# Grouping the value matmuls of two chunks in the attention loop of a one-core Macaron block

## What is computed

```
x = x + 0.5 * ffn(layernorm(x))      # 256 -> 1024, butterfly, gelu, butterfly, -> 256
Q, K, V = einsum('bsd,hkd->bhsk', layernorm(x), WQ / WK / WV)
scores = where(causal, einsum('bhqd,bhkd->bhqk', Q, K) / sqrt(16), -inf)
x = x + einsum('bhsv,hdv->bsd', softmax(scores) @ V, WO)
x = x + 0.5 * ffn(layernorm(x))
```

## Time and profile before

| | |
|---|---|
| median of 3 runs | 2121.79 us |
| the profiled execution, device time | 2122.12 us |
| its span from first to last instruction | 2120.3 us |
| mean granted TensorE clock | 0.988 |
| PE busy | 2033.0 us (96%) |
| DVE busy | 1680.3 us (79%) |
| ACT busy | 1350.4 us (64%) |
| POOL busy | 259.0 us (12%) |
| attention loop | 462.4 to 1884.2 us (first and last scores) |

### The profile page before, as it was taken

The page is one execution under the profiler, slowest core; times in us unless marked ns, Lnnn a source line. Parts: engine busy times, 40 slices in busy tenths (PEclk is TensorE's granted clock), DMA queues, the critical chain, the costliest instruction groups (busy, mean ns, idle before and its releaser), DMA issues.

```text
span 2120.3 us, 58107 instructions
## 1 busy us (share of the span) xinstructions
PE 2033.0 (96%) x23960; PEld 1207.5 (57%) x23960; DVE 1680.3 (79%) x3588; ACT 1350.4 (64%) x1592; POOL 259.0 (12%) x723
## 2 busy tenths in 40 slices
PE   1699999989999999999999999999999999999999
PEld 1476666555555555555555555555555555568887
DVE  6734444459999999999999999999999999635562
ACT  2423222238888888888888888888888888763222
POOL 8300000001111111111111111010110111100000
PEclk8799999999999999999999999999999999999999
DMA  7011211121211111111111111111111111101110
GB/s 202 22 48 47 86 52 51 47 61 44 51 42 45 41 43 49 42 46 41 44 47 42 46 43 44 46 42 46 43 44 45 42 46 33 50 24 60 60 40 21
DMA packets 89976, 104.19 MB, mean 49 GB/s; under 512 B 21264, under 2 KB 52592, under 8 KB 89456
## 3 DMA queue, kind: packets, MB, share of 16 engines
q1 hardware_dynamic: 89008, 100.23, 16.6%
q0 software_dynamic: 704, 0.25, 0.2%
HBM read 70.54 MB, written 29.36 MB: 47 GB/s over the span
## 4 chain that ended last, share of the span: by engine, by line
PE 92%; DVE 4%; ACT 2%; issue 1%; SPq 1%; DMA 0%; ACTq 0%; DVEq 0%
PE PS L1067 31%; PE PS L1189 30%; PE PS L1048 12%; PE PS L1025 6%; PE PS L1169 6%; PE PS L1120 3%; PE PS L1042 1%; DVE OA L781 1%; PE PS L991 1%; DVE BNS L718 1%; DVE OA L771 1%; ACT PG L606 0%; ACT L583 0%; SPq L367 0%; ACT OA L591 0%
## 5 line engine op out<-in xcount | busy, mean ns | idle before, releaser
L667 ACT ACTIVATE PG<-PS 128x1024 f32<-128x1024 f32 (+1 forms) x1152 | 1119.5, 978 | 248.0 <-PE PS L1169 186.3
L880 DVE TENSOR_REDUCE MXP<-PS 128x1 f32<-128x512 f32 x1792 | 1106.5, 686 | 35.7 <-PE PS L1067 34.8
L1067 PE MATMUL PS<-KT,QT 48*128 48x512 f32 (+3 forms) x2304 | 821.0, 431 | 5.6 <-DVE MXP L880 3.1
L1169 PE MATMUL PS<-QT,KT 50*128 50x512 f32 (+1 forms) x2304 | 810.0, 431 | 0.0
L1189 PE MATMUL PS<-PG,VH 128*17 128x128 f32 x16896 | 725.9, 276 | 0.1
L1189 PEld LDWEIGHTS PS<-PG,VH 128*17 128x17 f32 x16896 | 400.1, 96 | 414.5 <-issue 364.1
L1067 PEld LDWEIGHTS PS<-KT,QT 48*128 48x128 f32 x2304 | 345.8, 184 | 271.8 <-DVE MXP L880 129.9
L1169 PEld LDWEIGHTS PS<-QT,KT 50*128 50x128 f32 x2304 | 339.3, 184 | 10.3 <-issue 9.9
L876 DVE CUSTOM_DVE_ANT_0 PS<-PS,MASK 128x128 f32<-128x128 f32 (+3 forms) x512 | 249.9, 505 | 83.0 <-PE PS L1067 75.6
L551 POOL TENSOR_SCALAR_AFFINE_SELECT PG<-PG 128x128 f32<-128x128 f32 x512 | 137.3, 294 | 1005.4 <-ACT PG L667 1005.2
L1048 PE MATMUL PS<-MD,PG 128*128 128x256 f32 x1024 | 244.1, 388 | 4.9 <-DVE X L845 3.4
(11 more groups left out here) (101 smaller groups left out, 899.2 us busy)
## 6 DMA issues: line engine op xcount, KB each, us to landing
KT<-k_parts SPq DMA_DIRECT2D x256, 64.0 KB
QT<-q_parts SPq DMA_DIRECT2D x256, 64.0 KB
q_parts<-OA SPq DMA_DIRECT2D x16, 512.0 KB, 2.7
k_parts<-OA SPq DMA_DIRECT2D x16, 512.0 KB, 2.7
KT<-k_parts SPq DMA_DIRECT2D x256, 32.0 KB
QT<-q_parts SPq DMA_DIRECT2D x256, 32.0 KB
o_parts<-OS SPq DMA_DIRECT2D x128, 64.0 KB
OA<-o_parts SPq DMA_DIRECT2D x32, 256.0 KB
```

The costliest lines, as they stand in the source:

```text
L667: nc.scalar.activation(PB[n % 2][half][:, :, q0:TILE], PS[:, half * 1024:half * 1024 + 1024].rearrange("p (k q) -> p k q", k=2)[:, :, q0:T ...
L880: nc.vector.tensor_reduce(dst, bank(b), AX.X, ALU.max).then_inc(mx_red, 1)
L1067: mm(bank(4 + qs % 2 if b is None else b, w), NQ[0:SC, (BT * place(j) + qs) * P:(BT * place(j) + qs + 1) * P].bitcast(f32r), NK[0:SC, c * ...
L1169: last = mm(PS[:, (2 * half + k) * 512 + q0:(2 * half + k + 1) * 512], CK[0:SM, kb * P:(kb + 1) * P].bitcast(f32r), CQ[0:SM, place(j) * TI ...
```

## The change

The value records of a chunk's second half are no longer issued at the end of the step in which those of its first half are. They are issued a step later, immediately ahead of the value records of the next chunk's first half. Where a query tile ends (`ends_tile`), the second half stays at the end of its step. The counter `pv_done` becomes two, one for each half, and ACT's exponentials wait for the half of chunk n-2 whose buffer they write. Nothing is added or removed otherwise.

```
-        pv_done = sem("pv_done")
+        pv_done = [sem("pv_done0"), sem("pv_done1")]
...
+        def ends_tile(n):
+
+            return CH[n % NCH][1] == 0
...
-                    pool.wait_ge(pv_done, (h - 1) * NCH + CH.index((NT - 1, c)) + 1 + FREE_PB)
+                    pool.wait_ge(pv_done[1], (h - 1) * NCH + CH.index((NT - 1, c)) + 1 + FREE_PB)
...
-                act.wait_ge(pv_done, h * NCH + n + 1)
                 for half in range(2):
+                    act.wait_ge(pv_done[half], h * NCH + n + 1)
...
-                act.wait_ge(pv_done, h * NCH + LAST[j] + 1 + FREE_PB)
+                act.wait_ge(pv_done[1], h * NCH + LAST[j] + 1 + FREE_PB)
...
-                if half:
-                    last.then_inc(pv_done, 1)
+                last.then_inc(pv_done[half], 1)
...
                 ahead_maximum(n, 1)
+                if n > 1 and not ends_tile(n - 2):
+                    values(*divmod(n - 2, NCH), 1)
                 if n:
                     values(*divmod(n - 1, NCH), 0)
...
                 ahead_maximum(n, 3)
-                if n:
+                if n and ends_tile(n - 1):
                     values(*divmod(n - 1, NCH), 1)
```

More of the change, by code:

```diff
@@ L975, in _ @@
             pe.sem_inc(y_ps, 1)
-            pe.sem_inc(pv_done, FREE_PB)
+            for half in range(2):
+                pe.sem_inc(pv_done[half], FREE_PB)
             pe.wait_ge(a_up, 1)
```

## The result

The changed kernel takes 2227.02 us (median of 4 runs, 2219.74 to 2230.18), the kernel before 2121.67 (4 runs, 2121.38 to 2124.14): 105 us more, a ratio of 1.0489 with a 95% interval of 1.0462 to 1.0516. The profiled execution took 2225.89 us, with a span of 2224.1. The forecast was 2219, with a range of 2171 to 2261.

A forecast was written before the change was run, and what follows sets the result against it. PE's own rhythm was taken as the bound. 429 merged steps at +0.26 us give 111.5; minus 11.7, plus 3, minus 4 makes +99, lowered by 2: from 2122.1 to 2219 us, range 2171 to 2261.

The forecast's parts named there:

- The bound before: Loop before the change: PE's own rhythm bounds it, 2.44 us a step by pieces; DVE close behind with 2.40.
- The saving, 0.31: Each moved half on PE: 0.20 us from a first pair avoided plus 0.11 from joining a run of values.
- A merged step without any wait, 2.13 us: PE's time for a step with two value halves in one run, if nothing waits: 2.13 us.
- The wait, 0.58: Merged steps with maxima: fourth maximum in a row stalls 0.58 us for the first's reduction; step 0.26 us longer.
- The diagonal: 106 merged steps whose waiting maximum has 256 columns: -11.7 us; 106 whose waited-for maximum is diagonal: +3 us.
- The steps without maxima: 19 merged steps among the last 24 lose no time to banks: between no gain and -6 us, taken as -4.
- The sum: Whole kernel: 111.5 minus 11.7, plus 3, minus 4 gives +99 us, lowered by 2 for rounding: 2219 us.
- rival 4: Slower by under 45 or over 140 us without a clock fall, through unseen terms such as transposes in the bank round; 6%.
- 1 (faster): Saving stands, bank wait does not; DVE bounds at 2.40 us a step, 22 us less, 2100; needs wait below 0.31; 6%.
- 3 (the clock): PE without work about half a microsecond each step lowers the clock in the loop: about +110 us on top, 2330; 4%.

## Why the prediction was right, point by point

*The bound before.* PE's own rhythm, not DVE: right, but by little. Reductions of 128 columns shorten the old loop by only 5 us. In the plain steps M1's load started 0.10 us behind the end of M2's reduction on average, where 0.05 is the distance when it really waits: the order of before had 0.05 us to spare.

*The saving, 0.31.* Right: the joined half of values costs 1.00 - 0.56 = 0.44 (forecast 0.45), and the round with short reductions is as worked out. A merged step without any wait, 2.13 us, was not seen. In the last steps the length alternates between 1.00 + 1.15 = 2.15 and 1.00 + 1.33 = 2.33. The forecast named ACT's exponentials between the close scores as what could hold it up, and the weight loads of the scores in a longer step of that kernel show it:

```profile
1874.53 0.29 PEld L1174 LDWEIGHTS PS<-QT,KT 50*128 50x128 f32 x2 [0.38 <-ACT PG L671]
```

In the shorter step the same pause is 0.20 us.

*The wait, 0.58.* Right term by term: 0.02 and 0.70 for the reduction (forecast 0.04 and 0.69), 0.04 for the signal (0.05), 0.49 for a lone maximum (0.49, and the one that no row had shown), 2.71 for the round (2.71). From the starts of M2's weight loads in both traces, heads 1 to 15, I averaged the 204 merged steps off the diagonal and away from transposes: 2.701 us against 2.445. In the 87 kept steps of this kind it is 2.444 against 2.446.

*The diagonal.* Right: M1 with 256 columns makes it 2.585, 0.116 less (forecast 0.11); a diagonal M2 2.729, 0.028 more (0.03).

*The steps without maxima.* Forecast -4; 19 x 0.20 = 4 from two steps, and 3.3 by the loops of the kernel that is changed only there.

*The sum.* 97 us forecast, 103.6 in the loop. The term that was missing is the transposes, named only in rival 4 ("31, with a longer wait each") and given no price. Over the same heads the 28 merged steps next to a transpose that don't have a diagonal M2 grew by 0.42 us each, where the same steps away from a transpose give 0.26, or 0.14 with an M1 of 256 columns, 0.20 on average: (0.42 - 0.20) x 28 = 6 us, the difference. Leaving these steps out of the change gave back just what they had cost.

*The rivals.* 1 (faster) had the right mechanism for the saving and the right turning point: with reductions of 256 columns the stall worked out to 0.31 and the difference was 2 us. 3 (the clock) didn't come: the granted clock is 1.00 throughout. But its premise, PE busy some 80% with half a microsecond without work in each step, was wrong too: the half microsecond is a pause of the weight loads, and PE's matmul records cover 98% of the stretch, 1367 of 1400 us. What a larger pause would have done is not shown. What the Trainium skill says in "TensorEngine Tiling (Array Packing)", section Key Properties, that a change of tiling mode drains the engine, is in keeping with the saved part here (0.20 + 0.12 us a run), though no run separates a drain from another cost of changing between values and the rest; alone it would have given the wrong sign. What the Trainium skill says in "Perfetto Trace Analysis", section Matmuls, on rotating through PSUM banks so that their evacuation lies beside the next matmuls, was the rule that decided it. In a plain step the change loses 0.26 us and the saving of 0.32 with it, so the stall is 0.58 us.

No version that does all of the work beats the kernel before by what the runs can tell. The nearest is the change in the last 24 steps alone. A run of two halves keeps PE away from the maxima for 1.00 + 0.44 us; whether a fourth bank would let DVE work through that time was not tried, since scores, sums and maxima have all eight.

## What to carry to other kernels

When records are grouped to save a switch of the array, what stood between the groups is grouped too: count the users of each rotating buffer that now stand in a row, and where they outnumber the buffers, write down the round last user, evacuation, first user again, and compare it with the step. A moved instruction can be free itself and still have been the cover of someone else's wait. A quick test of such a round is to shorten the suspected engine's work in both orders: if only one order moves, the chain goes through it there.

## What was not expected of the hardware

The part ahead of the loop varies more than the loop. The first scores started at 454.6 us in one kernel's profiled execution and at 467.6 in another's, with the same code up to there but for the reductions' width:

```profile
L1174 PEld LDWEIGHTS PS<-QT,KT x2304: 182/184/191, 454.6 to 1874.9; 50*128 50x128 f32 x192
...
L1174 PEld LDWEIGHTS PS<-QT,KT x2304: 182/184/188, 467.6 to 1839.1; 50*128 50x128 f32 x192
```

The first is that of the changed order with 256 columns, the second with 128. Most of the 13 us goes with the granted clock (the third figure from the end of a row) ahead of the loop, here from 420 to 460 us in the same two executions:

```profile
420.00:460.00 40.00, 33.86 (x153) 21.66 (x152) 16.02 (x48) 12.32 (x21) 2.54 (x12) 0.91 0.18 60
...
420.00:460.00 40.00, 35.00 (x87) 20.93 (x88) 9.99 (x37) 5.51 (x10) 0.00 (x0) 0.66 0.03 12
```

A mean clock lower by 0.25 over 40 us is 10 us of full clock. The kernel before has 0.91 in that stretch too and started its scores at 462.4 us, so the clock isn't all of it, and what set it apart is not shown. The total of before itself ranged from 2115.9 to 2127.8 us over 23 runs, with mean granted clocks of 0.989 to 0.991 in the six shortest and 0.985 or 0.986 in the three longest; 0.005 of 2120 us is 11 us. The loops of before and of the counters alone agree within 0.1 us. A difference of a few us in such a kernel is read from the loop, not from the total.

Some executions enter the loop at the lower of TensorE's two clock levels, 1.2 GHz. The stretch 464 to 470 us of the kernel that is changed only at the end, and then of the kernel before, whose program is the same there (length, busy time of PE, PEld, DVE, ACT and POOL, granted clock, DMA):

```profile
464.00:470.00 6.00, 6.00 (x48) 2.67 (x46) 4.21 (x7) 2.85 (x4) 0.76 (x4) 0.50 0.38 72
```

```profile
464.00:470.00 6.00, 6.00 (x76) 3.54 (x80) 6.00 (x11) 4.80 (x6) 1.03 (x4) 1.00 0.44 74
```

At 0.50 PE gets through 48 matmul records in 6 us, at 1.00 through 76, and is shown as fully busy in both. Ahead of the loop's first maximum PE had waited 0.90 us for ACT in both, so that pause doesn't tell them apart. From 470 us to the end of the loop the clock was 1.00 in all profiled executions, with the pauses of weight loads of half a microsecond in the merged steps of the changed kernel too.
